# A gated attention and FFN block on one core: the instruction order of the attention phase, and the first FFN product in float32r passes

## The reference, cut

```python
x = x + tanh(g_xattn[0]) * attention(layernorm(x), ctx, ctx)     # 32 batches x 256 tokens x 256, 16 heads of 16
x = x + tanh(g_ffn[0]) * ffn0(layernorm(x))
x = x + tanh(g_xattn[1]) * dtw_align(ctx, layernorm(x))
x = x + tanh(g_ffn[1]) * ffn1(layernorm(x))

def ffn0(x):                       # w_fc 1024x256, w_proj 256x1024, u 1024x16, v 16x256, fast_b 16x16
    # bitlinear: weights replaced by sign {-1, 0, 1} times a scale per output row
    h = bitlinear(x, w_fc) + gate * (x @ v.T @ fast_b.T @ u.T)
    r = maximum(h, 0)
    return bitlinear(r * r, w_proj)
```

## Time and profile before

| | us |
|---|---|
| median of 3 runs | 2167.36 (2166.36 to 2174.5) |
| profiled execution | 2170.05 |
| its span | 2168.3 |

### The profile page before, as it was taken

The page is one execution under the profiler, slowest core; times in us unless marked ns, Lnnn a source line. Parts: engine busy times, 40 slices in busy tenths (PEclk is TensorE's granted clock), DMA queues, the critical chain, the costliest instruction groups (busy, mean ns, idle before and its releaser), DMA issues. The chain is left out here.

```text
span 2168.3 us, 37941 instructions
## 1 busy us (share of the span) xinstructions
PE 1573.3 (73%) x10467; PEld 1100.0 (51%) x10467; DVE 1575.6 (73%) x5042; ACT 1025.7 (47%) x2104; POOL 453.1 (21%) x589
## 2 busy tenths in 40 slices
PE   3689999999999999999999986233320037777876
PEld 1357676776767767677776765000000014445443
DVE  6556666676666766667666653799989968999997
ACT  0155555545555454555555552233320016777675
POOL 3111221212112121121111211000000024454453
PEclk9799999999999999999999998555555558889898
DMA  2434334343343433334343310222200022122210
GB/s 70 123 106 128 99 107 123 92 128 99 111 115 93 125 103 111 112 97 121 104 121 96 96 49 21 48 62 60 55 15 0 0 86 63 61 72 74 74 54 30
DMA packets 321893, 179.20 MB, mean 83 GB/s; under 512 B 92769, under 2 KB 317169, under 8 KB 321794
## 3 DMA queue, kind: packets, MB, share of 16 engines
q1 hardware_dynamic: 321794, 178.07, 28.8%
HBM read 122.91 MB, written 50.33 MB: 80 GB/s over the span
## 5 line engine op out<-in xcount | busy, mean ns | idle before, releaser
L761 DVE TENSOR_REDUCE nmax<-s 128x2 f32<-128x512 f32 x512 | 325.9, 683 | 120.3 <-PE s L377 119.7
L576 ACT ACTIVATE pt<-s 128x512 f32<-128x512 f32 x512 | 277.4, 600 | 11.3 <-PE s L392 11.2
L460 PE MATMUL wb<-x2T,wfcT 128*128 128x256 f32 x1024 | 241.9, 379 | 1.4 <-issue 1.4
L849 POOL TENSOR_TENSOR r<-rl 128x512 f32<-128x512 f32 x128 | 133.0, 1039 | 455.6 <-ACT rl L598 453.9
L460 PEld LDWEIGHTS wb<-x2T,wfcT 128*128 128x128 f32 x1024 | 184.9, 190 | 23.0 <-issue 1.7
L392 PE MATMUL s<-qst,kst 128*128 128x256 bf16 x1024 | 170.8, 276 | 16.1 <-ACT pt L576 8.6
L377 PE MATMUL s<-kst,qst 96*128 96x256 bf16 x1024 | 163.8, 276 | 21.0 <-DVE nmax L761 13.6
L404 PE MATMUL oacc<-pt,vw 128*32 128x256 f32 x2048 | 137.1, 385 | 45.9 <-ACT pt L576 45.9
L1362 PE MATMUL ph<-w1T,xqT 128*128 128x512 bf16 x384 | 119.0, 475 | 36.9 <-ACT xqT L1424 36.9
L1145 PE MATMUL gate<-diag,one 128*128 128x512 f16 x35 | 21.3, 608 | 171.3 <-DVE left L1220 171.3
L598 ACT ACTIVATE rl<-wb 128x512 f32<-128x512 f32 x128 | 76.3, 596 | 145.0 <-PE wb L460 145.0
(11 more groups left out here) (240 smaller groups left out, 3735.6 us busy)
## 6 DMA issues: line engine op xcount, KB each, us to landing
kst<-k_parts_dram SPq DMA_DIRECT2D x384, 64.0 KB, 2.6
qst<-q_parts_dram SPq DMA_DIRECT2D x384, 64.0 KB, 2.4
k_parts_dram<-kp SPq DMA_DIRECT2D x32, 384.0 KB, 4.7
q_parts_dram<-qp SPq DMA_DIRECT2D x32, 384.0 KB, 3.1
xin<-in_x_dram SPq DMA_DIRECT2D x32, 256.0 KB, 2.8
cT<-in_ctx_T_dram SPq DMA_DIRECT2D x32, 256.0 KB, 2.7
xres<-in_x_dram SPq DMA_DIRECT2D x32, 256.0 KB, 2.9
cin<-in_ctx_dram SPq DMA_DIRECT2D x32, 256.0 KB, 4.3
```

Source lines behind the costliest of these rows:

```text
L460: last = pe.matmul(B_FC[k][:, j, :], wfcT[:, c, f * P:f * P + P], x2T[:, c, :], start=(c == 0), stop=(c == C - 1))
L576: act.activation(pt[h % (2 * HPG)][:], s2[h % 2][:], ACT.Exp).then_inc(e["expd"], 1)
L761: v.tensor_reduce(nmax[:, T * h:T * h + T], s1[h % 2][:], AX.X, ALU.max, negate=True)\
L849: pool.tensor_tensor(r2[:], rl[:, k % 2], rl[:, k % 2], ALU.mult)\
```

## The change

Three things are changed.

First, the order. On PE, `scores2(i, 0, 4)` come earlier, `values(i, 0)` and `values(i, 1)` come earlier, the latter ahead of the turns of y and xh2, and `scores1(s, 6, 8)` too. On ACT the exponentials follow, `middle_part` of q and `values_copy` come behind `exps(i, 4, 6)`, and `exps(i, 6, 8)` behind those.

Second, the first FFN product. The weights `wfcT` hold only -1, 0 and 1, as float32r; their scale (`fscl`, one per output row) is applied in the relu. The activation is split into `x2h` (ACT's copy) and `x2l` (DVE's rest), and each pair of weight tile and part is one float32r pass. The low-rank term isn't folded into the weights any more: `low_rank` computes the 16 rank values, stacked in eight blocks of 16 rows (high and low parts), ACT and DVE split them into `lowt`, and one pass per output tile with `low2` adds them.

Third, small ones: `setup_weights` builds the new weights, the chains of `ctx_squares` and `normalise` use other semaphores.

```diff
-        wfcT = sb("wfcT", [P, C, F])
+        wfcT, fscl = sb("wfcT", [P, C, F], F32R), sb("fscl", [P, FT])
+        low1, low2 = sb("low1", [P, C, P], F32R), sb("low2", [P, F], F32R)
...
+            def low_rank(b):
+                w("x2T_cp", b.n + 1), w("x2_low", b.n + 1)
+                w("x1_res", b.n + 1), w("low_low", b.n)
+                for c in range(C):
+                    pe.matmul(B_NORMS[:, 1, :], low1[:, c, :], x2h[:, c, :], start=(c == 0), stop=False)
+                    last = pe.matmul(B_NORMS[:, 1, :], low1[:, c, :], x2l[:, c, :], start=False, stop=(c == C - 1))
+                last.then_inc(e["low_mm"], 1)
...
                 for j in range(2):
                     f = 2 * k + j
                     for c in range(C):
-                        last = pe.matmul(B_FC[k][:, j, :], wfcT[:, c, f * P:f * P + P], x2T[:, c, :],
-                                         start=(c == 0), stop=(c == C - 1))
+                        pe.matmul(B_FC[k][:, j, :], wfcT[:, c, f * P:f * P + P], x2l[:, c, :], start=(c == 0), stop=False)
+                        pe.matmul(B_FC[k][:, j, :], wfcT[:, c, f * P:f * P + P], x2h[:, c, :], start=False, stop=False)
+                    if f == 0:
+                        w("low_low", b.n + 1), w("low_cp", b.n + 1)
+                    last = pe.matmul(B_FC[k][:, j, :], low2[:, f * P:f * P + P], lowt[:], start=False, stop=True)
...
+            def low_copy(b):
+                w("low_mm", b.n + 1), w("fc_mm", 4 * b.n, 4 * NB)
+                act.activation(lowt[:], B_NORMS[:, 1, :], ACT.Copy).then_inc(e["low_cp"], 1)
+
             def bb_copy(b):
-                w("bb_mm", b.n + 1), w("d_part", b.n)
+                w("bb_mm", b.n + 1), w("low_mm", b.n + 2), w("d_part", b.n)
...
-                act.activation(rl[:, k % 2], B_FC[k][:], ACT.Relu).then_inc(e["relu"], 1)
+                for j in range(2):
+                    last = act.activation(rl[:, k % 2, j, :], B_FC[k][:, j, :], ACT.Relu,
+                                          scale=fscl[:, 2 * k + j:2 * k + j + 1])
+                last.then_inc(e["relu"], 1)
...
+            def low_half(b):
+                w("xh2_t", b.n + 1), w("x2T_cp", b.n + 1), w("fc_mm", 4 * b.n, 4 * NB)
+                v.tensor_tensor(x2l[:], B_XH2[:], x2h[:], ALU.subtract).then_inc(e["x2_low"], 1)
+
+            def low_rank_half(b):
+                w("low_mm", b.n + 1), w("low_cp", b.n + 1), w("bb_cp", b.n)
+                for q in (1, 3):
+                    rows = slice(32 * q, 32 * q + 32)
+                    last = v.tensor_tensor(lowt[rows, :], B_NORMS[rows, 1, :], lowt[rows, :], ALU.subtract)
+                last.then_inc(e["low_low"], 1)
...
                 if there(s):
                     maxima(s, 6, 8)
+                if there(z):
+                    low_half(z)
+                    low_rank_half(z)
                 if there(y):
                     distance_part(y)
...
-                pe.matmul(ps[3 + k % 2][:], fbv[:, c * P:c * P + P], uT[:, 512 * half:512 * half + 512],
-                          start=True, stop=True).then_inc(turned, 1)
+                    last = pe.transpose(ps[1 + k % 2][:, j * P:j * P + P], wfc[:, 4 * half + j, c * P:c * P + P],
+                                        o["ident"][:])
+                if k < 2:
+                    for j in range(4):
+                        last = pe.transpose(ps[3 + k][:, j * P:j * P + P], us[:, 4 * k + j, :], o["ident"][:])
+                last.then_inc(turned, 1)
```

More of the change, by code:

```diff
@@ L144, in attention_phase @@
         x1 = [sb(f"x1_{p}", [P, T, D]) for p in range(2)]
-        xh2, x2T = sb("xh2", [P, T, D]), sb("x2T", [P, C, S])
+        xh2 = sb("xh2", [P, T, D])
+        x2h, x2l = sb("x2h", [P, C, S], F32R), sb("x2l", [P, C, S], F32R)
+        lowt = sb("lowt", [P, S], F32R)
         rl = sb("rl", [P, 2, 2, S])
@@ L171, in attention_phase @@
                  "fc_mm", "pr_mm", "y_t", "bb_mm", "ab_mm", "s1_mm", "s2_mm", "av_mm",
-                 "xT_cp", "qh_cp", "kh_cp", "vw_cp", "onT_cp", "x2T_cp", "relu", "expd", "o_cp", "yT_cp", "bb_cp",
-                 "dist", "aa_half", "aa_sum",
-                 "ln1", "q_rem", "k_rem", "maxed", "max_split", "recip", "normed", "x1_res", "ln2", "x2_res", "ln3",
+                 "xT_cp", "qh_cp", "kh_cp", "vw_cp", "onT_cp", "x2T_cp", "x2_low", "low_mm", "low_cp", "low_low", "relu", "expd", "o_cp", "yT_cp", "bb_cp",
+                 "dist", "aa_sum",
+                 "ln1", "q_rem", "k_rem", "maxed", "max_split", "normed", "x1_res", "ln2", "x2_res", "ln3",
                  "d_part",
@@ L412, in turn_o @@
                 if half == 0:
-                    w("x2T_cp", b.n), w("qh_cp", b.n + 3), w("q_rem", b.n + 3)
+                    w("x2T_cp", b.n), w("x2_low", b.n), w("qh_cp", b.n + 3), w("q_rem", b.n + 3)
                 else:
@@ L476, in iteration @@
                     scores1(s, 2, 4)
+                if there(i):
+                    scores2(i, 0, 2)
                 if there(y):
@@ L480, in iteration @@
                     scores1(s, 4, 6)
+                if there(i):
+                    scores2(i, 2, 4)
                 if there(z):
@@ L485, in iteration @@
                 if there(i):
-                    scores2(i, 0, 2)
+                    values(i, 0)
+                    scores2(i, 4, 6)
                 if there(s):
                     values_proj(s)
+                    scores1(s, 6, 8)
                 if there(i):
-                    scores2(i, 2, 4)
-                    values(i, 0)
-                    scores2(i, 4, 6)
+                    scores2(i, 6, 8)
+                    values(i, 1)
                 if there(y):
@@ L496, in iteration @@
                     turn_xh2(z)
[L497 to L500, removed]
                 if there(y):
@@ L503, in iteration @@
                     row_norms(y)
+                if there(z):
+                    low_rank(z)
                 if there(i):
-                    values(i, 1)
                     scores2(i, 8, 10)
@@ L632, in iteration @@
                     ctx_squares(z)
+                if there(i):
+                    exps(i, 0, 4)
                 if there(a):
@@ L635, in iteration @@
                 if there(i):
-                    exps(i, 0, 2)
+                    copy_group(i, 0)
+                    exps(i, 4, 6)
+                if there(a):
+                    middle_part(a, "q_rem", qr, qp, "q_parts_mid")
                 if there(s):
@@ L639, in iteration @@
                 if there(i):
[L640 to L645, removed]
+                    exps(i, 6, 8)
+                    copy_group(i, 1)
                 if there(y):
@@ L649, in iteration @@
                     xh2_copy(z)
-                if there(i):
-                    exps(i, 6, 8)
+                if there(z):
+                    low_copy(z)
                 if there(y):
@@ L960, in _ @@
             pe.wait_ge(small, 96)
-            pe.matmul(ps[0][0:RANK, 0:D], fbT[:], vv[:], start=True, stop=True).then_inc(turned, 1)
+            for c in range(C):
+                last = pe.matmul(ps[0][:, c * RANK:c * RANK + RANK], vv[:, c * P:c * P + P], fbT[:], start=True, stop=True)
+            last.then_inc(turned, 1)
             pe.wait_ge(consts, 1)
-            pe.wait_ge(quant_p, 1)
+            pe.wait_ge(quant, 1)
             for k in range(4):
```

68 lines of the change are left out of this document (41 added, 27 removed).

## The result

| | before | after |
|---|---|---|
| median, us | 2167.43 (4 runs) | **2372.19** (2367.99 to 2374.65, 4 runs) |
| span of the profiled execution | 2168.3 | 2369.0 |
| mean granted clock | 0.871 | 0.835 |

The ratio is 1.0942, 95% interval [1.0917, 1.0966]: 9.4% slower. The prediction was 2261 (2190 to 2290). Its direction holds, its size doesn't: the time is 82 us above the range.

The account below looks back on a forecast made before the run. The prediction took PE as the bound, 94% busy in mid-attention. 28 iterations of +2.3 us waits and +1.3 us clock gave +101, less 3 for the drain and 4 for setup: 2261 us, range 2190 to 2290.

Parts of the forecast that it names:

- The FFN's first product: FFN on PE: float32r passes 0.117 us apart, fc(z,k) 1.25 us for 1.73, low_rank adds 0.55; 1.4 us less per iteration.
- What it adds on ACT and DVE: New FFN operations: low_copy 0.37 us, low_half 0.69, low_rank_half 0.7, split relu 0.85 in place of 0.60.
- step 1 and 2: PE works without a wait to 16.8 us, losing 1.5 us ahead of values(i,0); DVE's q_remainder ends at 18.42, before 17.93.
- Step 3: ACT, with middle_part(q) and values_copy ahead of exps(i,6..7), stops at q_rem until 18.46 us; exps(i,7) ends at 20.64.
- Step 4: PE waits 4.0 us for values(i,1), from 16.8 to 20.8 us.
- Step 5: PE's rest of the iteration: 16.6 us of work, waits of 0.6, 1.2, 1.3 and 0.5 us; iteration 41.0 us, +2.3.
- The clock: After PE's 4.0 us rest the clock falls, charged 1.3 us per iteration (0 to 3).
- The sum: 28 x (2.3 + 1.3) = +101 us, -3 for the four draining iterations, -4 for setup: +94, so 2261 us.
- A: Rival: the same wait at values(i,1), but PE's clock holds: 2225 us; chance 0.26.
- B: Rival: PE stays the bound and its waits don't grow: 2121 us; chance 0.12 together with smaller gains.
- D: Rival: gains and waits cancel, within 0.5% (11 us) of the kernel before; chance 0.05.
- C: Rival: the new fc misses 0.117 us, or the clock stays low all through the FFN: 2310 us; chance 0.07.

Follow-up runs that it names:

- order_only: The kernel before with the changed kernel's order on PE and ACT alone, its FFN, setup and DVE instructions kept: 2256.7 us, ratio 1.0406.
- after_shift8: The changed kernel with eight semaphore increments once ahead of DVE's program, its loop kept at 259 instructions but moved to 456-715: 2285.8 us, ratio 1.0528.
- ffn_only_trim: The new FFN in PE's and ACT's order of before, without DVE waits that other waits imply: 2170.5 us, ratio 1.0009 against the kernel before.
- after_trim: The changed kernel without DVE waits that other waits imply, DVE's loop body 251 instructions instead of 259: 2281.3 us, ratio 1.0519 against the kernel before.
- ffn_relu_whole: The new FFN in the order of before, with relu as one operation and the output rows' scale left out: 2141.8 us, ratio 0.9878.
- trim_shift12: The changed kernel without implied DVE waits, plus twelve semaphore increments ahead of the attention phase, DVE's body at 456-707: 2275.5 us, ratio 1.0493.
- before_pad8: The kernel before with eight semaphore increments more per iteration on DVE, body 260 instructions at 424-684: 2167.9 us, ratio 0.9995.
- pad8_shift24: The kernel before with 24 DVE semaphore increments ahead of the loop and eight per iteration in it, body at 448-708: 2245.5 us, ratio 1.0355.
- exps_first_trim: The changed kernel without implied DVE waits, with exps(i,6,8) ahead of middle_part(q) on ACT: 2168.8 us, ratio 1.0001 against the kernel before.
- ffn_act: New FFN in PE's old order, implied DVE waits removed; ACT's copy_group(0), exps(4,6) ahead of middle_part(q), distance(y) later, SP's store_d later: 2129.5 us, ratio 0.9821.

## Why the prediction was wrong, by its own steps

The +205 us, by the ratios of the experiments, each against the kernel before beside it: order_only 4.06% or 88 us; the new FFN in that order (after_shift8 less order_only) 1.22%, 26 us; the stop at the loop's top (after less after_shift8) 4.14%, 90 us. The sum is 204.

- **What bounds the kernel now**: held as to PE, the exponentials at values(0) (1.4 us) and the rule drawn from it, that PE's savings count only if no other chain becomes later. ffn_only_trim shows it at its purest.
- **The FFN's first product**: right. Passes start 0.12 us apart and fc(z,0) takes 783.29 - 782.04 = 1.25 us.
- **What it adds on ACT and DVE**: the relu pair 0.84 (taken 0.85), low_copy 0.38 (0.37), x2l 0.69 (0.69). low_rank_half 0.86 (0.7, bounds 0 to 1.5): two operations of 32 rows cost more than dt_'s two of 128, so the choice not to scale by rows was right.
- **The reordering, walked**: step 1 and 2 held. Step 3: exps(i,7) ends as said. Step 4: 3.68 us of idle, 3.8 from start to start, for 4.0. Step 5: idle of 1.3 to 1.4 for 1.2 at fc(z,0), and of 0.8 to 0.9 for 1.3 at scores2(12..13), which is 1.2 from start to start. With the clock 42.3 was walked and 42.4 is read in this iteration. But 38.66, from which the growth was counted, is the longer of two kinds of iteration: the mean is 38.5 before and 42.6 in after_trim, so the growth was 4.0 in place of 3.6.
- **The clock**: 1.3 charged, 1.4 read from values and turn.
- **The sum** is where it failed, twice. The small one: -3 for the four iterations that drain the pipeline. They add up to 130.7 us before, 137.3 in ffn_only_trim and 135.0 in after_trim: +4 to +7. With the relu whole (ffn_relu_whole) they take 127.9, which is about the -3. So the term counted the shorter FFN on PE and left out the split relu on ACT, for which PE waits there, at a clock of 0.92 over 145 us where before has 0.95 and ffn_relu_whole 0.97. The setup's -4 was right: the first turn of xhat starts at 52.90 and stood at 57.74.
- The large one is a **missing term**: no line of the sum was about the jumps of the hardware loop, so DVE's stop there stood at nothing. I read the iteration from the earlier trace rows and multiplied by 28, as if all were alike, and the change's 15 instructions more on DVE were counted as busy time only. Each jump costs 6.5 us of DVE and PE's clock behind it. A pair of iterations takes 50.0 + 43.4 = 93.4 us, and 2 x 42.6 = 85.2 in after_trim: 11 x 8.2 = 90, as measured. With 90 for the stop, 7 for the drain (4 in place of -3) and 12 for the iterations (28 x 0.4) the forecast of 2261 becomes 2370, against 2372.2.
- **The rivals**: A falls by the clock, B by the sign, D by the size. C gave 2310 (its own sum, 2261 + 28 x 2, is 2317) and was the only one on the side of the result, but by a mechanism that isn't there: the passes run at 0.12 us, and the clock is back at 1.00 by 776, ahead of the FFN. No rival was about the instruction stream.

**Open**: why the stop is 6.5 us when the body starts at 448, and 2.8 when it starts at 440; where exactly the borders lie; and the differences of 4 to 6 us between after_shift8, after_trim and trim_shift12 (waits on DVE, or its body's place).

## What to carry to other kernels

Before you multiply one iteration's saving or cost by their number, ask what each engine does at the loop's back edge: count each engine's instructions in the body, padding and waits too, and look for an `issue` wait that comes once per pass and for packets on the instruction queue.

When engines are in-order, find the step that is late (here q_rem) and keep everything that the bound engine wants next ahead of its consumer; one move on ACT was worth 113 us here, and the same rule applied to before gave 1.4%. A saving on PE is worth what the other engines' chains leave of it, so price it together with the order on them, and price a pipeline's drain by itself: there the split relu on ACT cost 9 us in four iterations.

## What the runs showed of the hardware that I had not expected

- A loop body of 260 DVE instructions costs nothing at one place (before_pad8) and 77 us at another (pad8_shift24 against the kernel before: 2245.5 against 2168.4), with identical work: 11 stops of up to 7.0 us, and 115 instruction packets instead of 60. Bodies of 259 and 276 did both as well; those of 244 and 251 never stopped where they were tried.
- The stop's cost differs: 30.5 us for eleven with a body of 276 from 440 on, 68.8 with one of 260 from 448 on. Start and length weren't separated.
- A DVE operation of 32 rows and 256 columns took 0.42 us, and so did one of the same kind with 128 rows (`on`, TENSOR_TENSOR from PSUM): fewer rows bought nothing.
- A rest of 3.68 us on PE was followed by some 3 us at 1.2 GHz, while single rests of 1.0 to 1.5 us in the loop (exps_first_trim, ffn_act) left the clock at 1.00. In the last stage, where rests come close together, it fell after 1.55 and 0.99 us.
